# Order of the chunks in the mixing phase: all channel-mixing chunks first, then the twelve shared-expert chunks in one sequence

## The reference, cut to what matters

```python
x = x + 0.5 * _L0_ffn_ref(_layernorm(x), ...)
x = x + _L0_attn_ref(_layernorm(x), ...)      # mixing: time mixing, then channel mixing
x = x + 0.5 * _L0_ffn_ref(_layernorm(x), ...) # experts, second pass
...
# channel mixing, in _L0_attn_ref
kk = (h * cm_mk + hh * (1 - cm_mk)) @ Wkey.T
kv = jax.nn.silu(kk) @ Wval.T
x = x + sigmoid(...) * kv
# experts, in _L0_ffn_ref
logits = x @ gate_w
scores = jax.nn.softmax(logits, axis=-1)
topk_w, topk_idx = jax.lax.top_k(scores, K)
g = silu(einsum('td,edh->teh', x, w_gate)) * einsum('td,edh->teh', x, w_up)
routed = einsum('teh,ehd,te->td', g, w_down, comb)
shared = silu(x @ sw_gate) * (x @ sw_up) @ sw_down
```

## Time and profile before

| | us |
|---|---|
| three runs, median (lowest, highest) | 1470.75 (1470.04, 1474.9) |
| span of the profiled execution | 1467.1 |
| PE busy | 1164.5 (79%) |
| DVE busy | 753.7 (51%) |
| POOL busy | 582.5 (40%) |
| ACT busy | 486.5 (33%) |

### The profile page before, as it was taken

One profiled execution on the slowest core, in us unless ns is written; L12 is line 12 of the kernel. 1 busy time (PEld: TensorE's weight loads), 2 busy tenths in 40 slices (PEclk: granted clock), 3 DMA queues, 4 the chain that ended last, 5 costly groups with the idle time before them and its releaser, 6 DMA issues.

```text
span 1467.1 us, 19455 instructions
## 1 busy us (share of the span) xinstructions
PE 1164.5 (79%) x5926; PEld 946.3 (65%) x5926; DVE 753.7 (51%) x2317; ACT 486.5 (33%) x934; POOL 582.5 (40%) x571
## 2 busy tenths in 40 slices
PE   3799993578889797499836549999987777599994
PEld 3687771356578685377625339999755455499993
DVE  5653343454544534235553417477866663275665
ACT  2222322354633422134323114444414221244441
POOL 3660342211203012212577630376622666204766
PEclk9999996799979887799857869999998859799997
DMA  9512448500000030475332256788611222468997
GB/s 329 228 55 72 151 123 281 198 0 1 1 1 29 6 156 34 172 261 174 112 125 90 90 188 182 229 275 266 204 33 36 89 90 90 140 187 246 280 279 223
DMA packets 125154, 210.03 MB, mean 143 GB/s; under 512 B 15280, under 2 KB 104752, under 8 KB 123184
## 3 DMA queue, kind: packets, MB, share of 16 engines
q1 hardware_dynamic: 100480, 141.64, 29.0%
q0 software_dynamic: 24576, 67.14, 14.7%
HBM read 129.56 MB, written 101.19 MB: 157 GB/s over the span
## 4 chain that ended last, share of the span: by engine, by line
PE 53%; POOL 16%; issue 13%; DVE 9%; ACT 6%; DMA 4%; SPq 0%; POOLq 0%; ACTq 0%; DVEq 0%
PE ps L814 16%; POOL xd L582 14%; PE ps L824 11%; PE ps L785 5%; PE ps L732 5%; PE ps L744 3%; PE ps L956 3%; PE ps L795 3%; PE ps L1058 2%; ACT xnt L1165 1%; DMA yd<-yo 1%; DMA G<-yd,slot_of 1%; PE ps L963 1%; POOL G L596 1%; PE ps L678 1%
## 5 line engine op out<-in xcount | busy, mean ns | idle before, releaser
L596 POOL DMA_INDIRECT G<-yd,slot_of x256 | 249.0, 973 | 385.5 <-DMA yd<-yo 289.2
L582 POOL DMA_INDIRECT xd<-xnt,slot_of x256 | 255.7, 999 | 199.0 <-issue 105.9
L814 PE MATMUL ps<-WE,xT 128*128 x1016 | 189.2, 330 | 0.3
L1298 ACT ACTIVATE xT<-ps 128x512 f32<-128x512 f32 (+1 forms) x168 | 99.4, 591 | 250.4 <-PE ps L785 249.6
L1783 DVE TENSOR_TENSOR hid<-hid,ps 128x192 f32<-128x192 f32 (+2 forms) x168 | 65.4, 389 | 214.8 <-ACT hid L1317 213.5
L814 PEld LDWEIGHTS ps<-WE,xT 128*128 128x128 f32 x1016 | 164.8, 193 | 1.1 <-issue 0.7
L785 PE MATMUL ps<-ident,xd_in 128*128 128x128 f32 x664 | 104.8, 281 | 61.0 <-DMA xd_in<-xd 55.7
L1790 DVE COPY yo<-ps 128x512 f32<-128x512 f32 (+1 forms) x168 | 114.8, 684 | 65.1 <-PE ps L824 65.1
L1762 DVE SCALAR_TENSOR_TENSOR XT<-G,wt,XT 128x256 f32<-128x256 f32 x256 | 123.6, 483 | 45.7 <-DMA G<-yd,slot_of 33.7
L785 PEld LDWEIGHTS ps<-ident,xd_in 128*128 128x128 f32 x664 | 85.1, 145 | 80.7 <-issue 62.6
L1184 ACT ACTIVATE S<-ps 128x512 f32<-128x512 f32 (+1 forms) x72 | 42.8, 595 | 268.6 <-PE ps L732 267.5
(11 more groups left out here) (225 smaller groups left out, 1989.1 us busy)
## 6 DMA issues: line engine op xcount, KB each, us to landing
xd_in<-xd SPq DMA_DIRECT2D x164, 256.0 KB, 4.1
yd<-yo SPq DMA_DIRECT2D x164, 256.0 KB, 2.9
WE<-w SPq DMA_DIRECT2D x8, 1280.0 KB, 7.2
W0E<-w0e SPq DMA_DIRECT2D x2, 4864.0 KB, 24.2
xd<-xnt,slot_of POOLq DMA_INDIRECT x256, 2.4
G<-yd,slot_of POOLq DMA_INDIRECT x256, 3.6
XT<-x_in SPq DMA_DIRECT2D x4, 512.0 KB, 6.8
out<-XT SPq DMA_DIRECT2D x16, 128.0 KB, 3.4
```

The source lines that it names most:

```text
L582: nc.gpsimd.indirect_dma_start(xd[f // 2][:, :], bass.IndirectOffsetOnAxis(ap=slot_of[:, t, k:k + 1], axis=0), xnt[:, t, :], None).then_in ...
L596: nc.gpsimd.indirect_dma_start(G[:, n % G_RING, :], None, yd[f // 2][0:min(ly.early[t] * 2, ly.TILES) * P, :], bass.IndirectOffsetOnAxis(a ...
L814: last = mm(dst, xT[:, q % 2, a, k, :], flat[:, bass.ds(expert[2 * q + a] + k * 2 * ly.H, 2 * ly.H)], start=(k == 0), stop=(k == KD - 1))
L1298: fn(xT[:, q % 2, 0:m].rearrange("p a k t -> p (a k t)"), ps[:, TX, 0:m * D], ACT.Copy).then_inc(TL.xT, 1)
```

## The change

Stages fall from eight to six, and no stage holds shared chunks any more. The twelve shared chunks of the second pass stand in a list of their own, DRAIN, which PE, ACT and DVE go through after the stages, one chunk per step d. The routing steps of the last block (and what was left of block 2's: score, choice, rank, slots) are placed at given steps of that list. In it PE holds one chunk, not two, between `gate_up` and `down` (`lagging(1)`), and DVE's `finish` is one chunk behind, not two. POOL's power for the last block and the scatters of blocks 2 and 3 follow its loop over the stages.

```diff
-    add(("c", 0), "c", None, 0, HID, (2, 3))
-    add(("c", 1), "c", None, 1, HID, (2, 3))
-    add(("c", 2), "c", None, 2, HID, (2, 3))
-    add(("s", 1, 0), "s0", 1, 0, SH0, (2,))
-    add(("c", 3), "c", None, 3, HID, (2, 3))
-    for b in range(1, NB):
+    for b in range(NB):
+        add(("c", b), "c", None, b, HID, (2, 3))
+    for b in range(NB):
         add(("s", 1, b), "s0", 1, b, SH0, (2,))
...
 def stage_chunks(s):
-    run = lambda *key: RUN[key][0] if key in RUN else []
-    return (run("c", s - 2) if s >= 2 else []) + (run("s", 1, s - 4) if s >= 4 else [])
-
-
-STAGES = 8
-STREAM = [ch for s in range(STAGES) for ch in stage_chunks(s)]
+    return RUN["c", s - 2][0] if 2 <= s < 2 + NB else []
+
+
+STAGES = 2 + NB
+DRAIN = [ch for b in range(NB) for ch in RUN["s", 1, b][0]]
...
                 if 0 <= r < NB:
                     scatter(1, r)
+            inverse(F_NORM[1], NB - 1)
+            for b in range(STAGES - 4, NB):
+                scatter(1, b)
...
                         lagging(LAG)
-                    lagging(LAG if s + 1 < STAGES and stage_chunks(s + 1) else 0)
+                for d, ch in enumerate(DRAIN):
+                    step(ch)
+                    if d == 2:
+                        turn(F_NORM[1], NB - 1, xnt, A_BANK)
+                        rank(1, NB - 2, B_BANK + 1)
+                    if d == 3:
+                        logits(1, NB - 1, A_BANK)
+                    if d == 5:
+                        rank(1, NB - 1, A_BANK + 1)
+                    lagging(1)
+                lagging(0)
...
+                for d, ch in enumerate(DRAIN):
+                    silu(ch)
+                    hidden(stream.pop(0))
+                    stream.append(ch)
+                    if d == 0:
+                        score(1, NB - 2, B_BANK)
+                    if d == 1:
+                        rows(F_NORM[1], NB - 1, XT[:, tiles_of(NB - 1), :])
+                    if d == 2:
+                        high(1, NB - 1, A_BANK)
+                    if d == 4:
+                        score(1, NB - 1, A_BANK)
...
+                for d, ch in enumerate(DRAIN):
+                    prod(ch)
+                    stream.append(ch)
+                    summed.append(ch)
+                    low_hidden(stream.pop(0))
+                    finished(1)
+                    if d == 0:
+                        dve.wait_ge(CK.sum, GROUP["c", NB - 1] + 1)
+                        stats(F_NORM[1], NB - 1, XT[:, tiles_of(NB - 1), :])
+                        offsets(F_NORM[1], NB - 1)
+                    if d == 1:
+                        chosen(1, NB - 2)
+                    if d == 2:
+                        low(1, NB - 1, A_BANK)
+                    if d == 3:
+                        slots(1, NB - 2, B_BANK + 1)
+                        zed(1, NB - 1, A_BANK)
+                    if d == 4:
+                        chosen(1, NB - 1)
+                    if d == 6:
+                        slots(1, NB - 1, A_BANK + 1)
+                for ch in stream:
+                    low_hidden(ch)
+                finished(0)
```

More of the change, by code:

```diff
@@ L1000, in mixing @@
                                 pe.wait_ge(A0.aff2, b2 + 1)
-                            elif r == NB - 1:
-                                pe.wait_ge(RT.mask, NB + NB)
                             pe.wait_ge(A0.sr, min(b2, NB))
```

## The result

The changed kernel takes 1464.63 us (median of six runs, 1462.44 to 1466.72), the kernel before, run beside it, 1471.74 (1470.04 to 1474.9): a ratio of 0.9949, interval 0.9934 to 0.9964, or 7.1 us less. The forecast was 1475.7, so its sign was wrong. The range, from 1465, missed the time by 0.4 us.

What follows compares the result with a forecast made beforehand. It took PE's 13.83 us wait for scattered rows before the expert pairs as the largest hole. -8.4 (pair 0 earlier) - 1.7 (first pairs) + 10.2 + 4.8 (clock) = +4.9, so 1475.7 us; range 1465 to 1486.

Steps and rivals of the forecast that it cites:

- the mechanism: Shared chunks in the list: with one chunk of lag `down` waits for DVE's remainder, 6.45 us per chunk, before 4.47.
- the round price: Lag of one in the list: twelve times 1.98, 24 us of added waiting, called the main cost of the change.
- the scatter and the weights: Ahead of pair 0: scattered rows loaded at 584, 17 us ahead of need; expert weights at 568, cover 33 us.
- the signs given beforehand: Profile after: `gate_up` 6.4 to 6.5 us apart, no wait for scattered rows, pair 0 at 600 to 617, clock 0.86.
- Right in kind: the list: First shared chunk to pair 0, step by step at the high clock: 88.95 us, pair 0 8.4 earlier.
- the clock: PE's clock falling behind waits in the list: 10.2 us for three long waits plus 4.8 for four short ones.
- The three long waits: PE's waits at d = 1, 4 and 7 of the list: 3.4 us of clock loss each, range 5.1 to 13.8 together.
- the four waits of 2.0: PE's waits of 2.1 us at d = 6, 8, 9 and 11: 1.2 us of clock loss each, 0 to 14.4 together.
- The rival "faster": Whole kernel: closed hole before the expert pairs decides, clock loss under 5.7 us, 1465.8 or 1460.6 us; chance 0.20.
- within 0.3%: Whole kernel: the same sum with a clock loss of 6 to 14 us, 1466.4 to 1475.1 us; chance 0.34.
- the start of the list: First shared chunk at 512.8: "c" chunks start 13.98 us earlier, less 1.22 for one more `finish` pass; 12.75 earlier.
- the first pairs: Pair 0's transposes to `up` of pair 1: 7.1 us in place of 8.8, 1.7 gained.

Runs made afterwards that it cites:

- e_lag2: The changed kernel with two chunks, not one, between `gate_up` and `down` in the list from the second chunk on; 1447.86 us against 1470.42 for the kernel before.
- before_again: The kernel before, unchanged, run and profiled a second time; 1474.77 us.
- e_lag2_split: The changed kernel with two chunks of lag and DVE's `offsets` of block 3 one step later; ratio to before 0.9806, on another chip 0.9834.
- e_order_only: The kernel before with only the new order of chunks, keeping its stages, routing places and lag of two; 1453.28 us, ratio to before 0.9884.
- e_warm: The changed kernel with products without use in PE's waits in nine steps of the list; ratio to before 1.0010.

## Why the prediction was wrong

**Right: the mechanism.** Two chunks to one cost 6.46 per chunk in the list, forecast 6.45. In a steady chunk after, from `gate_up` at 585.29, the remainder ends at 590.15, and `down` starts at 590.21, 4.92 behind it, where the sum from the earlier trace rows had 4.97. Only the round price, 24 us for twelve chunks, was too high: e_lag2 gives 17.7. The DVE pieces:

```profile
588.86 0.69 DVE L1743 TENSOR_TENSOR S<-S,ps 128x512 f32<-128x512 f32 x1 [5.17 <-ACT S L1191]
589.47 0.68 DVE L1748 TENSOR_TENSOR HL<-S,HL 128x512 fp32r<-128x512 f32 x1
```

**Right: the scatter and the weights.** The last slots are written at 572.60, and the eight scatters follow, the last from 584.83:

```profile
573.06 0.95 POOL L578 DMA_INDIRECT xd<-xnt,slot_of  x1 [13.75 <-DVE slot_of L1692]
```

SP loads the rows from 587.29, and they take 3.0: about 17 us ahead of need, as forecast. The expert weights are issued at 557.00 and take 15.7, in place of 14.3: 35 ahead. One of the signs given beforehand did not follow from the steps themselves: the last slots were to come 25 us before the last shared sum, while the steps put them at 568 and 601.5, 33 us apart; measured are 35.

**Right in kind: the list.** Measured against forecast, step by step from d = 0: 6.46 (6.5), 10.04 (8.6), 7.48 (6.45), 6.86 (7.0), 9.06 (8.7), 7.69 (6.45), 7.45 (6.45), 11.23 (9.9), 6.55, 6.46, 6.46 (6.45 each) and 9.52 (9.55) to pair 0. At the steps without a clock loss the two agree to 0.15 us. What is over comes to 6.3 of 95.26, nearly all of it in pieces that ran at the lower clock.

**Wrong: the clock, +15.0 forecast, +6.3 measured.** This is the step that failed. The three long waits were there, of 3.75, 3.62 and 4.37 us (forecast 3.6, 3.65, 4.85), but cost 2.2, 1.6 and 1.3 in place of 3.4 each, by the starts of the slow pieces; 5.1 for 10.2. Of the four waits of 2.0 only the first, at 564.98, cost anything: 1.0 us, in place of 1.2 each. In the window 565:567.5 the clock stands at 0.55, and in 583:590, with two such waits, at 1.00. Together 6.1, and 6.3 with 0.2 by which the steps themselves were too short: 8.7 less than forecast.

The price of 3.4 came from rows in which the clock stayed low for some 7 us. Read in windows of half a microsecond, it is at 0.50 before from 493.5 to 500.5, around the row at 494.54. In the list only the first wait had as long a stretch, 524.5 to 531; the others had half of it, 551.5 to 555, 565 to 568.5 and 575.5 to 578.5. Part of the slow work there was free as well: the `gate_up` at 567.51, 0.6 us longer than at the high clock, ran while DVE was at the slots. Why the stretches were shorter no run shows. The mean of the three costs is 1.7, the prediction's lower bound, which is known only afterwards. The rival "faster" starts from it, but by its own condition (a loss under 5.7) it did not come true in the list: -10.1 + 6.3 = -3.8 belongs to "within 0.3%", with its loss of 6 to 14. What took the time past that, and past the range, is the next step.

The Trainium skill, TensorE: Matmul & The Clock Gate, section "A second HAM failure mode: psum-queue depth-cycling", says that brief idling between groups of matmuls, if it comes often enough, makes the clock swing and costs throughput. It gives no price for one pause; that every one of the four would cost 3.6 was the prediction's own reading. In this list one of the four did cost something, 1.0 us.

**Wrong: the start of the list, -12.75 forecast, -16.17 measured.** From the turn to the list are 95.43 us before and 79.26 after. The order of work gives what I worked out: the wait there grew to 6.00 (4.75 + 1.22). The other 3.4 is clock again, 27.57 for 31.01, as told at before_again. The forecast didn't have it: it is a gain by luck, and without it the change would have brought 3.0 us, not 6.4. I had carried the cold pieces of before over unchanged, as if the instructions behind a longer wait had to run at the same clock.

**Wrong by 0.8: the first pairs.** Pair 0 to `up` of pair 1 is 7.92, forecast 7.1, since the clock falls at `up` of pair 0 after all (4.16, at 609.90) behind short waits of 1.15 and 0.78.

The misses add up: 8.7 + 3.4 - 0.8 = 11.3, which takes the forecast +4.9 to the measured -6.4. The rest of the program carried the shift on: the spans differ by 2.8, of which 3.1 is the difference ahead of the turn, and 0.5 us came back behind the phase.

**Open.** What makes the clock fall behind one pause and not behind a like one isn't settled, nor why it fell at three places of e_lag2_split's list on one chip and not on the other. With two executions of that kernel, the chip and chance can't be told apart.

## What to carry to other kernels

Price a shorter lag apart from the reordering that comes with it: here the order and the earlier routing brought 23 us, the lag took 18 back, and with the lag at two the kernel is 1.5% faster than before. A clock loss read from one place can't be carried over to an edited sequence, and in one of three kernels not even to a second execution; where a forecast's sign hangs on it, take the smallest of the rows as seriously as their mean, and put more chance on the rival that goes with it. A stretch between two fixed instructions tells more of such an edit than the medians do, once a second profile has shown how well it repeats: to 0.1 us in two kernels here, to 4.6 us in a third.

## What was unexpected of the hardware

The kernels before and after show the same slow pieces in both of their profiled executions (31.01 and 31.03 us, 95.26 and 95.31), while a neighbouring kernel with nearly the same pauses shows others. That is no rule: the kernel of e_lag2_split had lists of 73.73 and 78.31 us on two chips, with equal waits. A longer wait was even followed by less loss: after 6.00 and 5.37 us the stretch took 27.57 and 27.84, after 4.75 it took 31.01.

The clock also fell with PE at work, at or behind the 24 narrow logits products: before (2.91 for the `down` behind them), e_lag2 (4.30 for the `gate_up` that follows), e_order_only (4.59) and e_warm (4.52); not in the changed kernel, where `down` behind the logits at 539.20 takes 1.68. Products without use, put in the pauses of e_warm, did not keep it up there either.
